# Two attention products on GpSimd, one unit earlier: a graph layer and a Mamba layer on one Trainium2 core

## The reference: what is computed

```python
Xw = X @ Wv + bv
sj = Xw @ aw[:d, 0]
si = Xw @ aw[d:, 0]
e = jax.nn.leaky_relu(sj[:, None, :] + si[:, :, None] + ab[0], negative_slope=0.2)
alpha_matrix = A * jnp.exp(e)
transition = alpha_matrix / (jnp.sum(alpha_matrix, axis=-1, keepdims=True) + 1e-12)
...
h = dA * h + (d_t * u_t)[..., None] * B_t[:, None, :]
y_t = jnp.einsum('bds,bs->bd', h, C_t)
```

## Time and profile before

| what | value |
|---|---|
| median of three runs | 3722.97 us (3718.68 to 3727.8) |
| the profiled execution | 3724.0 us, span 3722.2 us |
| busy, TensorE / VectorE / ScalarE / GpSimd | 92% / 94% / 80% / 93% |
| granted clock of TensorE, mean over the span | 0.989 of full |
| instructions | 43792 |

### The profile page before, as it was taken

The page is one execution under the profiler, slowest core; times in us unless marked ns, Lnnn a source line. Parts: engine busy times, 40 slices in busy tenths (PEclk is TensorE's granted clock), DMA queues, the critical chain, the costliest instruction groups (busy, mean ns, idle before and its releaser), DMA issues.

```text
span 3722.2 us, 43792 instructions
## 1 busy us (share of the span) xinstructions
PE 3433.3 (92%) x11130; PEld 1959.2 (53%) x11130; DVE 3496.5 (94%) x2813; ACT 2975.3 (80%) x6611; POOL 3456.8 (93%) x1767
## 2 busy tenths in 40 slices
PE   5899999999999999999999999999999999999887
PEld 3555555555555555555555555555555555555443
DVE  0499999999999999999999999999999999999998
ACT  2588878888888888888888888888888888888774
POOL 0299999999999999999999999999999999999998
PEclk9899999999999999999999999999999999999999
DMA  3111101111101111100111110111110111110110
GB/s 112 53 56 59 59 9 53 56 58 58 59 9 53 56 59 58 58 29 33 56 58 58 59 44 18 58 56 58 58 59 4 58 56 58 59 54 9 46 51 9
DMA packets 50720, 183.68 MB, mean 49 GB/s; under 512 B 7356, under 2 KB 33220, under 8 KB 42086
## 3 DMA queue, kind: packets, MB, share of 16 engines
q1 hardware_dynamic: 48898, 174.17, 12.1%
q10 hardware_dynamic: 1636, 7.83, 0.5%
HBM read 164.15 MB, written 17.83 MB: 49 GB/s over the span
## 4 chain that ended last, share of the span: by engine, by line
POOL 46%; issue 30%; PE 18%; DVE 4%; ACT 2%; POOLq 1%; DMA 0%; SPq 0%; DVEq 0%; ACTq 0%
POOL st L438 31%; POOL st L429 9%; PE y_ps L796 8%; PE d_ps L853 3%; POOL delta L411 3%; POOL du_sb L419 2%; DVE st L988 2%; PE g L816 1%; PE g L947 1%; DVE st L976 1%; PE d_ps L864 1%; ACT dec L505 1%; POOL rstd L396 1%; POOL att L376 1%; POOLq L193 1%
## 5 line engine op out<-in xcount | busy, mean ns | idle before, releaser
L438 POOL TENSOR_TENSOR st<-st,bc 128x1024 f32<-128x1024 f32 x1024 | 2404.9, 2366 | 97.8 <-DVE st L988 97.2
L988 DVE TENSOR_TENSOR_SCAN st<-dec,st 128x1024 f32<-128x1024 f32 x1024 | 2308.8, 2272 | 11.9 <-ACT dec L505 7.1
L796 PE MATMUL y_ps<-st,ident 128*128 128x512 f32 x4096 | 1932.5, 605 | 158.2 <-POOL st L438 156.8
L505 ACT ACTIVATE dec<-delta,decay 128x254 f32<-128x254 f32 x4096 | 1696.2, 466 | 239.6 <-DVE st L988 236.6
L796 PEld LDWEIGHTS y_ps<-st,ident 128*128 128x128 f32 x4096 | 747.3, 191 | 984.4 <-issue 657.5
L976 DVE TENSOR_TENSOR st<-du,bc 128x1024 f32<-128x1024 f32 x736 | 882.4, 1199 | 12.9 <-PE y_ps L796 12.4
L429 POOL TENSOR_TENSOR st<-du_sb,bc 128x1024 f32<-128x1024 f32 x288 | 681.8, 2368 | 0.1
L833 PE MATMUL d_ps<-xnT,wxz 128*128 128x256 f32 x1024 | 249.4, 387 | 71.4 <-DVE u L1013 70.7
L1013 DVE SCALAR_TENSOR_TENSOR u<-d_ps,chan,u 128x250 f32<-128x250 f32 (+2 forms) x768 | 305.9, 465 | 7.8 <-ACT u L553 7.8
L553 ACT ACTIVATE u<-d_ps,bconv,chan 128x256 f32<-128x256 f32 x256 | 130.0, 558 | 215.7 <-PE d_ps L833 215.7
L833 PEld LDWEIGHTS d_ps<-xnT,wxz 128*128 128x128 f32 x1024 | 191.7, 191 | 156.1 <-DVE u L1013 105.0
(11 more groups left out here) (113 smaller groups left out, 2560.0 us busy)
## 6 DMA issues: line engine op xcount, KB each, us to landing
bc<-bc_dram SPq DMA_DIRECT2D x64, 2048.0 KB, 9.8
xg<-x_dram SPq DMA_DIRECT2D x32, 256.0 KB, 11.4
x_dram<-xg SPq DMA_DIRECT2D x32, 256.0 KB, 2.0
last_x<-x_dram SPq DMA_DIRECT2D x32, 256.0 KB, 2.6
out_dram<-last_x SPq DMA_DIRECT2D x32, 256.0 KB, 2.1
bc<-w_inT_dram ACTq DMA_DIRECT2D x1, 4096.0 KB, 13.9
adjt<-adjT_dram SPq DMA_DIRECT2D x32, 128.0 KB, 11.1
bc<-w_out_dram ACTq DMA_DIRECT2D x1, 2048.0 KB
```

The lines of the kernel that those rows point to most:

```text
L438: nc.gpsimd.tensor_tensor(st[:, sl, :, :, :], st[:, sl, :, :, :], bc[:, p, 1, SU * q:SU * q + SU, None, :].to_broadcast([P, SU, 2, T]), AL ...
L505: a = nc.scalar.activation(dec[:, v % 2, s, j, :].rearrange("p (b t) -> p b t", b=PAIR)[:, :, 1:], delta[:, p, 2 * i + j, :].rearrange("p ...
L796: mm = nc.tensor.matmul(y_all, ident[:, :], st[:, sl, s, :, :].rearrange("p j t -> p (j t)"), start=False, stop=(q == Q - 1 and s == SU - ...
L988: nc.vector.tensor_tensor_scan(h, dec[:, v % 2, :, :, :].rearrange("p s j t -> p (s j t)"), h, 0.0, ALU.mult, ALU.add).then_inc(S["scanned ...
```

## The change

The two products of `weights` are issued in the body's unit 21 and not 22. `weights` is called at the head of a unit, ahead of the unit's `c_product`; so it stood between products 21 and 22 and now stands between the inject of unit 24 (issued in unit 20) and product 21.

```diff
@@ -53,7 +53,7 @@
 Z_FOLDS = {(-2, 6): 4, (-1, 1): 5, (-1, 3): 6, (-1, 5): 7}
 Z_BIAS = {(-1, 7): 2, (-1, 9): 3}
 EDGE_STEP = 8
-ALPHA = 12
+ALPHA = 11
 FIRST_STEP, SECOND_STEP, RSTD_STEP = 0, 8, 9
```

## The result

The changed kernel takes 3732.9 us (median of 22 runs, 3722.62 to 3743.25), the kernel before 3723.9 us (22 runs, 3718.62 to 3729.8). The ratio is 1.0022, 95% interval [1.0015, 1.0028]: slower by 8 to 9 us, a small loss that is clear of the noise. I had forecast 3721.5 us, a gain of 1.5. The time lies in my range, 0.1 us from its end, and within the 0.3% that I called no change, but its sign is the wrong one, and the spread of the runs, 20.6 us against 11.2 before, says that something comes and goes.

A forecast was written before the change was run, and what follows sets the result against it. VectorE (94% busy) and GpSimd (93%) were read as bounding, with GpSimd behind at the weights and clock falls on TensorE delaying VectorE. Terms 0 + 0 + 0 - 1.5 against the median 3722.97 gave 3721.5 us, range 3708 to 3733.

The forecast's parts named there:

- The moved instructions: GpSimd's two weights instructions, 1.59 us, start earlier; their input from ScalarE is ready in time, so no new wait: cost 0.
- product 21: On GpSimd it ends 1.59 us later, but neither TensorE's sum of unit 21 nor VectorE's inject of unit 29 suffers: cost 0.
- the alpha sum: On TensorE it comes after the sum of unit 22, so alpha being ready 2.3 us earlier gains nothing: gain 0.
- TensorE's gaps: Idle gaps of 1.37 and 1.91 us become 2.96 us ahead of unit 21's sum and 0.33 us ahead of unit 22's.
- One fall at the sum of unit 21 costs at most 1.15: A clock fall at TensorE's sum of unit 21 would be partly absorbed, making it at most 1.15 us late.
- The second place: VectorE's convolution taps waited 1.58 us for ScalarE behind matmuls at clock 0.50; expected to stand against a free drift.
- the governor: TensorE's clock is decided on its own beat; the kernel drifts until hit, a pair without a fall being 1.3 us too short.
- The mean stays at 221.86 whatever one fall costs: Mean length of two bodies stays 221.86 us, as long as a pair's falls can add up to 1.3 us.
- the 222.7 that was to show me wrong: Upper limit for the mean of two bodies, in us; the forecast counts as wrong over it or under 221.1.
- The gain of 1.5 us: The clock term on TensorE, the only nonzero one: 1.5 us gained.
- two wrong ends: Bounds of the clock term: 17.5 us gained if all ten falls vanish, 16 us lost if all 29 bodies fall.
- The rival that the clock would fall in every body: TensorE's 2.96 us gap draws the clock down each time, at 1.15 us: 3739 us, chance 0.08.

The follow-up runs named there:

- the kernel filled at both places: Changed kernel with zero-weight matmuls, three ahead of the sum of unit 21 and two in unit 4: 3705.62 us; kernel before with five likewise: 3706.23 us.
- with unit 4 filled: Two zero-weight matmuls in unit 4 only, ahead of the projection of u: changed kernel 3722.44 us, ratio 0.9988; kernel before 3725.07 us, ratio 0.9996.
- the second set: Changed kernel run again, nothing more changed, against the kernel before on the same chip: 3734.33 us, ratio 1.0028.
- the third: Changed kernel run once more, nothing more changed, against the kernel before on the same chip: 3726.11 us, ratio 1.0008.
- the weights alone: Three zero-weight matmuls ahead of the sum of unit 21 in the changed kernel: 3719.22 us; ahead of units 21 and 22 in the kernel before: 3714.51 us.

## Why the prediction was wrong

*The moved instructions, product 21, the alpha sum: cost 0.* Right, and shown: no wait at the weights outside the lead-in, and 3705.62 against 3706.23 us for the two orders once the clock no longer falls in the loop, with loops 0.3 us apart.

*TensorE's gaps.* Right: I had 2.96 and 0.33 us. Measured are 2.96 and 2.95 ahead of the sum of unit 21, and 0.33 ahead of that of unit 22 in the kernel filled at both places.

*"One fall at the sum of unit 21 costs at most 1.15".* Right for the fall of single length: the body of 1253.03 takes 110.75 us, and the like body of 1252.53 in the kernel before, without a fall, took 1362.30 - 1252.53 = 109.77, 0.98 us less. Wrong as a bound. A fall that begins ahead of the sum, 3.05 to 3.3 us behind the start of the weights, lasted 6.8 us in every loop body of the changed kernel's profiles that has one, and cost about 2 us there (113.02 against 111); two that began at 3.49 us and, with unit 4 filled, at 3.44 us lasted 3.4. This is the first step that failed: a cost of at most 1.15 us that came to about 2, and to 4.0 with the fall in unit 4. I priced the fall with its length of before, though its start had moved to where TensorE is idle. The kernel before had shown that falls can be longer, from 519.2 to 526.0 in the earlier trace rows, and at what price (its starts of the weights around it):

```profile
472.75 0.74 POOL L376 TENSOR_TENSOR att<-att,x1k 128x256 f32<-128x256 f32 x1
...
585.66 0.72 POOL L376 TENSOR_TENSOR att<-att,x1k 128x256 f32<-128x256 f32 x1
```

That body took 112.91 us, 1.9 more than its like.

*The second place.* I had named it as part of the governor that holds the mean. In truth it adds: in a dear body the fall at the weights is followed by one in unit 4, and the two cost 4.0 us together (114.86 us); filling the second place takes away one part.

*"The mean stays at 221.86 whatever one fall costs".* Wrong, and this is the step on which the forecast of 3721.5 us stood. The kernel before does come back to that mean: with unit 4 filled, four pairs take 2144.25 - 1256.89 = 887.36 us, 221.84 each.

```profile
1256.89 0.72 POOL L378 TENSOR_TENSOR att<-att,x1k 128x256 f32<-128x256 f32 x1
...
2144.25 0.75 POOL L378 TENSOR_TENSOR att<-att,x1k 128x256 f32<-128x256 f32 x1
```

The changed kernel's ordinary pair, 221.6 us, is a little below it, but what follows is no small correction: the next one leaps to 225.5. In the eight bodies above the mean is 223.57, and over the 27 bodies of the loop 223.06 (3011.30 / 13.5), above the 222.7 that was to show me wrong; the other two profiles of the changed kernel have 222.52 and 222.01, the kernel before 222.07. In place of a gain of 1.5 us stands a loss of 8 to 9, of 13.4 in the loop of the profiled run. That it is the phase against the clock's own beat which decides between the cases fits the regular pattern, the spread between runs and the Trainium skill's statement below, but no run here set the phase, so this part is argued and not shown.

*The gain of 1.5 us* was a choice near the middle of two wrong ends, with no row behind its sign. Its upper end counted ten falls to be gained, where the loop of the kernel before has eleven at the weights; at one of them rowsum waits only 0.04 us. That the median still lies in the range is luck, since the mechanism that was to hold the time there did not; in the second set it was 3734.33. The rival that the clock would fall in every body, priced at 3739 us, had the right sign and the right engine: the profiled run's 3741 is near it, the median is half way. It was wrong in its price and its count too: at the weights 20 of the 29 bodies have a fall, most for less than 1 us, and the five dear ones pay 20 of the 33 us.

The Trainium skill's rule, "TensorE: Matmul & The Clock Gate", in "HAM oscillation — how this bites in real kernels", that idle gaps between bursts put the clock back, told the sign. The trace agrees in part: with the gap of 2.96 us some falls are longer (6.8 us) than with those of 1.37 and 1.91 us (3.4 us), but not in every body. What the Trainium skill says on the same page in "What's actually happening", that the activity is watched on a beat of its own, agrees with falls that come in a pattern over several bodies.

## What to carry to other kernels

When a change moves a wait on one engine, list the idle gaps that it makes or merges on TensorE, and look at the granted clock at every place where TensorE is idle for microseconds in a row, not only at the one that is edited: here a loss of 2 us at one place was in many bodies followed by a fall at another. Price a fall of the clock by its longest instance in the trace, too. A few matmuls with zero weights, added where TensorE idles anyway, are a cheap test of such a theory and here a gain of 0.5%. Fill all the places at once: the weights alone gave 0.28 and 0.36%, unit 4 alone 0.12 and 0.04%.

## What the runs showed of the hardware that was not expected

Matmuls with zero weights held the granted clock at 1.00 through both places (1352 to 1366 and 1400 to 1412 above). The granted clock fell in the kernel before behind gaps of 1.37 and 1.91 us with a sum of 1.98 us between them, in 11 of the 28 bodies of the loop, and it stayed down for 3.4, 6.8 or 10.1 us while TensorE worked without a pause, as from 1844.6 to 1854.7. And two kernels whose instructions on TensorE are the same can differ in the spread of their runs: 11.2 against 20.6 us at first, 14.0 against 21.8 in the second set, though not in the third (15.9 against 15.8).
